# GpSimd's order in the first feed-forward: the next group's statistics ahead of this group's residual sums, with two once-normalised tiles

## The chip, the cores and the metric

The kernel runs on one core of a Trainium2 chip. The metric is the device time of one launch in microseconds (us); less is better. Five engines work side by side, each through its own list of instructions and in order: TensorE (PE in the rows, PEld for its weight loads), VectorE (DVE), ScalarE (ACT), GpSimd (POOL) and SyncE (SP), which starts transfers. They meet only at semaphores. SBUF is the on-chip memory that all of them read, and PSUM is the memory in which TensorE leaves its sums.

## The reference

A tensor x of 64 tiles, each of 128 tokens by 128 features, goes through four blocks of cross-attention and feed-forward. Each of the eight steps is added to x. The change touches the second step only, the first feed-forward (`L0_ffn`). It normalises an input that the caller has already normalised, so the normalisation is done twice:

```python
h0 = _layernorm(x)                       # once-normalised
# _L0_ffn_ref(h0, ...):
residual = h0
h = (h0 - mean(h0)) * rsqrt(var(h0) + EPS) * ln_gamma + ln_beta   # twice-normalised
w1 = dequant(fc1_q, fc1_scales)          # 128 x 512
y = silu(h @ w1 + fc1_bias)
z = y @ dequant(fc2_q, fc2_scales) + fc2_bias
x = x + (residual + 0.5 * z)
```

So three things are added to x in this step: the once-normalised tile h0 (the residual), half of the bias, and half of the product. The halving is folded into the weights and the bias beforehand.

## The kernel before

x stays in SBUF as one tile `x` of 128 partitions (tokens) by 64 by 128. Each step walks over it in 16 groups of 4 tiles (`GROUPS`, `GT`), 512 columns at a time. The first feed-forward is the class `SiluFfn`, whose walk is in its parent `Hidden`. For one group g the work is this, in the order of the data:

- VectorE takes the means and variances of the four tiles (`vector_stats`, L186 and L191) into `ln_mean_var`. There is only one such buffer.
- GpSimd turns them into the factors of both normalisations (`pool`, six small instructions of 128x4, L204 to L210). L205 and L210 are powers of -1/2. Each of the six waits for the one before. The results are in `ln_rstd` and `ln_rstd2` (the rows call both ln_rstd).
- VectorE writes the once-normalised tile `f_once` (L239, four instructions of 128x128) and from it the twice-normalised tile `z` (L244, four more). This is `vector_z`.
- TensorE transposes z (`turn_z`, L985), ScalarE copies it out with gamma and beta (`f_zt`, L1051), and VectorE splits it into a high part (L1086, a cast) and a low part (L1088, a difference of two SBUF tiles).
- TensorE makes the hidden layer from high and low parts (`hidden`, L86 to L88, twelve products for a group), ScalarE applies silu (L1062), and TensorE makes the output (`output`, L1013).
- GpSimd adds `f_once` to x (L221) and then the bias (L224). This is `pool_bias`. VectorE adds the output to x (`add_output`, L1099), which reads one operand from PSUM.

The groups are staggered. In one turn of the loop TensorE takes hidden(g+1), the transposes of z(g+2) and output(g). VectorE takes z(g+2), the statistics of g+3, the split of g+2 and the sum of output(g), in this order. The order is written out by hand in `tensor_walk`, `vector_walk`, `scalar_walk` and `gpsimd`, and nothing else sets it. GpSimd takes one group after the other, first `pool(g)` and then `pool_bias(g)`, so its factors for the next group wait behind the two sums of this one. VectorE may not write `f_once` again before L221 has read it (the semaphore `once_added`).

`for_groups` is the helper that unrolls a loop by two so that buffers in pairs have a constant index `par`. The loop over GpSimd's groups used a plain loop before.

Of the kernel before, what the change touches and what calls it, by code (L numbers as in the profile page):

```python
# [25 lines left out]
F32 = mybir.dt.float32  # L26
F32R = mybir.dt.float32r
BF16 = mybir.dt.bfloat16
ALU = mybir.AluOpType
# [4 lines left out]
P = 128  # L34
# [4 lines left out]
GT = 4  # L39
GROUPS = BATCH // GT  # L40
# [6 lines left out]
class Counter:  # L47


    def __init__(self, sem, credit=0):  # L50
        self.sem, self.credit, self.base = sem, credit, credit
# [21 lines left out]
def for_groups(eng, body, peel=1):  # L73


    with eng.Fori(0, GROUPS // 2 - peel) as i:
        body(2 * i, 0, 2 * peel)
        body(2 * i + 1, 1, 2 * peel)
    for left in range(2 * peel - 1, -1, -1):
        body(GROUPS - 1 - left, 1 - left % 2, left)  # L80
# [15 lines left out]
class Core:  # L96
# [24 lines left out]
    def sb(self, ctx, name, shape, dt):  # L121
        return ctx.enter_context(self.nc.sbuf_tensor(name, shape, dt))
# [24 lines left out]
class Chain:  # L147
# [5 lines left out]
    def step(self, eng, ins):  # L153
        ins.then_inc(self.claim.sem, 1)
        self.n += 1
        eng.wait_ge(self.claim.sem, self.claim.at(self.n))


class LayerNorm:
# [51 lines left out]
            if self.once is None:  # L211
                step(eng.tensor_tensor(c.rstd[:, :], c.rstd[:, :], c.rstd2[:, :], ALU.mult))

    def pool_bias(self, eng, g):
        if self.bias is None:
            return
        c = self.core
        eng.wait_ge(self.z_ready.sem, self.z_ready.at(GT * g + GT))
        xg = c.x[:, ds(GT * g, GT), :]
        if self.once is not None:  # L220
            eng.tensor_tensor(xg, xg, self.once[:, :, :], ALU.add).then_inc(self.once_added.sem, 1)  # L221
            eng.wait_ge(self.once_added.sem, self.once_added.at(g + 1))
            eng.sem_inc(self.pool_seen.sem, 1)
        eng.tensor_tensor(xg, xg, self.bias[:, :].unsqueeze(1).broadcast_to([P, GT, P]), ALU.add)\  # L224
           .then_inc(self.bias_added.sem, 1)

    def vector_z(self, eng, g):

        c = self.core
        eng.wait_ge(self.rstd_step.sem, self.rstd_step.at(self.pool_steps * g + self.pool_steps))  # L230
        for k in range(GT):
            xk = c.x[:, ds(GT * g + k, 1), :].rearrange("p a d -> p (a d)")
            if self.once is None:
                eng.tensor_scalar(self.dest(g, k), xk, c.mean_var[:, k, 0:1], c.rstd[:, k:k + 1],
                                  ALU.subtract, ALU.mult).then_inc(self.z_ready.sem, 1)
                continue
            if k == 0 and not (isinstance(g, int) and g == 0):
                eng.wait_ge(self.once_added.sem, self.once_added.at(g))
            eng.tensor_scalar(self.once[:, k, :], xk, c.mean_var[:, k, 0:1], c.rstd[:, k:k + 1],  # L239
                              ALU.subtract, ALU.mult).then_inc(self.once_ready.sem, 1)  # L240
        if self.once is not None:
            for k in range(GT):
                eng.wait_ge(self.once_ready.sem, self.once_ready.at(GT * g + k + 1))
                eng.tensor_scalar(self.dest(g, k), self.once[:, k, :], c.rstd2[:, k:k + 1], None, ALU.mult)\  # L244
                   .then_inc(self.z_ready.sem, 1)


# [56 lines left out]
class SavedLayerNorm(LayerNorm):  # L304
# [11 lines left out]
    def pool(self, eng, g):  # L316
        pass

    def vector_z(self, eng, g):
        for k in range(GT):  # L320
            b = GT * g + k
            eng.tensor_scalar(self.dest(g, k), self.core.x[:, ds(b, 1), :].rearrange("p a d -> p (a d)"),
                              self.batch.mean_of(b), self.batch.rstd_of(b), ALU.subtract, ALU.mult)\
               .then_inc(self.z_ready.sem, 1)


class Phase:
# [5 lines left out]
    def gpsimd(self, eng):  # L333
        pass
# [605 lines left out]
class Hidden(Phase):  # L940
# [161 lines left out]
    def vector_walk(self, eng):  # L1102
        self.ln.vector_z(eng, 0)
        self.split_zt(eng, 0, 0)
        self.ln.vector_stats(eng, 1)
        self.ln.vector_z(eng, 1)
        self.apply_gates(eng, 0, 0)
        self.split_zt(eng, 1, 1)
        self.ln.vector_stats(eng, 2)

        def step(g, par, left):
            if left > 1:
                self.ln.vector_z(eng, g + 2)
            if left > 2:
                self.ln.vector_stats(eng, g + 3)
            if left > 0:
                self.apply_gates(eng, g + 1, 1 - par, (0, 1))
            if left > 1:
                self.split_zt(eng, g + 2, par)
            if left > 0:  # L1120
                self.apply_gates(eng, g + 1, 1 - par, (2, 3, 4))
            self.add_output(eng, g, par)

        for_groups(eng, step, 2)
        eng.wait_ge(self.added.sem, self.added.at(GROUPS))
        eng.sem_inc(self.done.sem, 1)

    def gpsimd(self, eng):
        eng.wait_ge(self.before.sem, self.before.at(1))
        self.ln.pool(eng, 0)  # L1130
        self.wait_bias(eng)
        self.ln.pool_bias(eng, 0)
        with eng.Fori(1, GROUPS) as g:
            self.ln.pool(eng, g)
            self.ln.pool_bias(eng, g)


class SiluFfn(Hidden):
# [5 lines left out]
    def __init__(self, core, before):  # L1144
        self.core = core
        self.i = {k[len("L0_ffn_"):]: v for k, v in core.ins.items() if k.startswith("L0_ffn_")}
        C = self.F // P
        sb, ctx = core.sb, ExitStack()
        self.affine = sb(ctx, "f0_gb", [P, 2], F32)
        self.b1 = sb(ctx, "f0_b1", [P, C], F32)  # L1150
        self.bias = sb(ctx, "f0_b2", [P, P], F32)
        self.q1 = sb(ctx, "f0_q1", [P, self.F], mybir.dt.int32)
        self.q2 = sb(ctx, "f0_q2", [P, C, P], mybir.dt.int32)
        self.s1 = sb(ctx, "f0_s1", [P, self.F], F32)
        self.w2 = self.s2 = sb(ctx, "f0_w2", [P, C, P], F32)
        self.w1 = [sb(ctx, f"f0_w1{h}", [P, self.F], F32R) for h in ("hi", "lo")]
        self.once = sb(ctx, "f0_once", [P, GT, P], F32)
        self.setup(before, [P] * C, ACT.Silu, LayerNorm(core, True, self.bias, once=self.once))
        self.buffers(ctx, "f0_")
        ctx.close()  # L1160
        self.loaded = core.claim("w_loaded", 16 * 8)
        self.prep = core.claim("prep_step", 6)
# [1385 lines left out]
```

## Time and profile before

| | us |
|---|---|
| median of 3 runs | 3059.89 |
| lowest and highest of them | 3056.15 and 3061.35 |
| span of the profiled execution, first to last instruction | 3055.5 |
| TensorE's mean granted clock in it, share of full speed | 0.917 |

A run's time is that of the launch. The span leaves out what lies before the first and behind the last instruction. The profiled execution's own launch time is not listed apart; its span is 0.65 us under the fastest of the three runs and 4.4 us under their median. A time worked out from the trace is therefore a difference of two spans, and it is added to the median.

Of this span the first feed-forward takes some 160 us: its first statistics start at 729.86 and its last sum into x ends at 891.87. A row of the timeline gives the start, the length, the engine, the line, the operation, output and inputs, the number of instructions that are merged into the row, and in brackets how long the engine was idle before it and whom it waited for. A merged row names the start of its first instruction, and its length runs to the end of its last.

### The profile page before, as it was taken

What the parts mean: (1) busy time and instruction counts of PE and PEld (TensorE: products, weight loads), DVE (VectorE), ACT (ScalarE), POOL (GpSimd) and SP (SyncE); (2) the same over time, 40 slices, a digit from 0 to 9 for tenths busy, and PEclk for the clock granted to TensorE, in tenths of its full rate; (3) what the DMA queues carried; (4) which work ended last, traced back from release to release, by engine and by line L of the source; (5) the groups of instructions that cost most, each with busy time, mean ns of one, the idle gap of its engine ahead of it and who ended that gap; (6) DMA issues with size and microseconds to landing.
All of it is one profiled execution on the core that took longest, in us unless ns stands there. A gap on an engine that the chain in (4) does not pass through costs nothing.

```text
span 3055.5 us, 58066 instructions
## 1 busy us (share of the span) xinstructions
PE 2622.0 (86%) x17377; PEld 2252.0 (74%) x17378; DVE 2034.5 (67%) x4748; ACT 1653.6 (54%) x3673; POOL 426.9 (14%) x572
## 2 busy tenths in 40 slices
PE   6999999996879999413589999999966997869998
PEld 5888888884768988301378888888865786668887
DVE  4888888886647777679846666666665444655554
ACT  4666666663336666225566666666623433425554
POOL 1011100111630111230000000000000102302223
PEclk9999999998999999755779999999968998969999
DMA  4000000000000000000000000000000000020000
GB/s 105 1 0 0 0 0 0 0 1 15 0 13 1 0 0 0 8 0 0 21 5 1 0 0 0 0 0 0 1 9 0 0 0 4 0 85 8 14 14 22
DMA packets 36054, 25.06 MB, mean 8 GB/s; under 512 B 10300, under 2 KB 32332, under 8 KB 35852
## 3 DMA queue, kind: packets, MB, share of 16 engines
q1 hardware_dynamic: 35980, 24.12, 2.9%
q8 instruction: 41, 0.67, 0.1%
q14 instruction: 33, 0.27, 0.0%
HBM read 19.92 MB, written 4.19 MB: 8 GB/s over the span
## 4 chain that ended last, share of the span: by engine, by line
PE 75%; DVE 9%; issue 6%; ACT 4%; POOL 3%; DMA 1%; DVEq 1%; POOLq 0%; SPq 0%; ACTq 0%
PE ps_o L637 11%; PE ps_t L614 11%; PE ps_s L626 11%; PE ps_p L86 6%; PE ps_p L88 6%; PE ps_p L87 6%; PE ps_t L2214 2%; PE ps_o L2214 2%; PE ps_o L1013 2%; PE ps_s L86 2%; PE ps_t L1013 2%; ACT a_vals_t L734 1%; PE ps_s L88 1%; PE ps_s L87 1%; DVE f_rng L1414 1%
## 5 line engine op out<-in xcount | busy, mean ns | idle before, releaser
L854 DVE TENSOR_REDUCE a_sm<-a_e 128x16 f32<-128x1232 f32 (+1 forms) x192 | 234.6, 1222 | 401.7 <-ACT a_e L762 400.8
L754 ACT ACTIVATE a_val<-ps_t 128x512 f32<-128x512 f32 (+1 forms) x448 | 223.2, 507 | 400.5 <-PE ps_t L614 399.0
L637 PE MATMUL ps_o<-a_val,a_pt 128*128 128x128 f32 (+2 forms) x3200 | 390.6, 276 | 4.0 <-DVE x L868 2.6
L637 PEld LDWEIGHTS ps_o<-a_val,a_pt 128*128 128x128 f32 (+2 forms) x3200 | 382.5, 192 | 12.3 <-DVE x L868 3.1
L626 PE MATMUL ps_s<-a_keys,a_zt 128*128 128x308 f32 (+1 forms) x1024 | 365.0, 488 | 4.6 <-DVE a_e L846 2.4
L734 ACT ACTIVATE a_vals_t<-ps_p 128x308 f32<-128x308 f32 x616 | 264.4, 430 | 84.2 <-PE ps_p L88 84.0
L734 ACT ACTIVATE a_keys<-ps_p 128x308 f32<-128x308 f32 x614 | 263.2, 429 | 58.5 <-PE ps_p L88 58.4
L614 PE MATMUL ps_t<-ident,a_e 128*128 128x128 f32 (+1 forms) x1600 | 265.2, 278 | 32.6 <-DVE a_e L862 16.0
L626 PEld LDWEIGHTS ps_s<-a_keys,a_zt 128*128 128x128 f32 x1024 | 185.0, 190 | 117.5 <-issue 101.3
L614 PE MATMUL ps_t<-ident,a_vals_t 128*128 128x128 f32 (+1 forms) x1600 | 251.8, 273 | 9.5 <-ACT a_val L754 9.5
L86 PE MATMUL ps_p<-ct_hi,a_vo_hi 96*128 (+1 forms) x616 | 241.5, 392 | 5.6
L86 PE MATMUL ps_p<-ct_hi,a_mt_hi 96*128 (+1 forms) x614 | 243.3, 396 | 0.0
L754 ACT ACTIVATE a_pt<-ps_t 128x512 f32<-128x512 f32 (+1 forms) x448 | 226.1, 507 | 29.9 <-PE ps_t L614 29.5
L862 DVE TENSOR_TENSOR a_e<-a_e,a_rs 128x1232 f32<-128x1232 f32 (+1 forms) x192 | 235.7, 1228 | 6.6
L614 PEld LDWEIGHTS ps_t<-ident,a_e 128*128 128x128 f32 (+1 forms) x1600 | 190.8, 139 | 56.8 <-issue 24.7
L762 ACT ACTIVATE a_e<-a_e 128x1232 f32<-128x1232 f32 (+1 forms) x192 | 204.7, 1066 | 5.0 <-DVE a_e L846 4.8
L204 POOL TENSOR_TENSOR ln_var<-ln_mean_var,eps 128x4 f32<-128x4 f32 x96 | 24.9, 260 | 1302.6 <-DVE ln_mean_var L191 1255.6
L614 PEld LDWEIGHTS ps_t<-ident,a_vals_t 128*128 128x128 f32 (+1 forms) x1600 | 190.0, 138 | 19.5 <-ACT a_val L754 18.5
L88 PE MATMUL ps_p<-ct_hi,a_mt_lo 96*128 (+1 forms) x614 | 188.9, 308 | 0.0
L87 PE MATMUL ps_p<-ct_lo,a_mt_hi 96*128 (+1 forms) x614 | 188.6, 307 | 0.0
L88 PE MATMUL ps_p<-ct_hi,a_vo_lo 96*128 (+1 forms) x616 | 187.2, 304 | 0.0
L87 PE MATMUL ps_p<-ct_lo,a_vo_hi 96*128 (+1 forms) x616 | 187.2, 304 | 0.0
(358 smaller groups left out, 5651.9 us busy)
## 6 DMA issues: line engine op xcount, KB each, us to landing
x<-in_x_dram SPq DMA_DIRECT2D x8, 512.0 KB, 7.5
out_dram<-x SPq DMA_DIRECT2D x8, 512.0 KB, 3.2
f_wf<-in_L_ffn_W_dram SPq DMA_DIRECT2D x1, 2048.0 KB
f_b<-in_L_ffn_b_dram SPq DMA_DIRECT2D x1, 2048.0 KB, 13.4
ctx_rows<-in_ctx_dram SPq DMA_DIRECT2D x4, 462.0 KB
a_wq<-in_L_xattn_Wq_dram SPq DMA_DIRECT2D x2, 512.0 KB
a_wo<-in_L_xattn_Wo_dram SPq DMA_DIRECT2D x2, 512.0 KB
f_w<-in_L_ffn_W_dram SPq DMA_DIRECT2D x3, 256.0 KB
```

The costliest lines, as they stand in the source:

```text
L86: eng.matmul(out, lhs[0], rhs[0], start=start, stop=False)
L87: eng.matmul(out, lhs[0], rhs[1], start=False, stop=False)
L88: return eng.matmul(out, lhs[1], rhs[0], start=False, stop=stop)
L614: mm = eng.transpose(c.ps_t[0:w, slot, (i % GT) * P:(i % GT + 1) * P], src[:, P * i:P * i + w], c.ident[:, :])
L626: eng.matmul(o, zt, keys[:, h0:h0 + nh, :], start=True, stop=True)\
L637: mm = eng.matmul(c.ps_o[:, (k % 2) * P:(k % 2 + 1) * P], self.pt[0:w, i, :], self.val[0:w, i, :], start=(i == 0), stop=(i == self.chunks ...
L734: eng.activation(dst[:, par, :, h, :], src.rearrange("p (b k) -> p b k", b=GT), ACT.Copy)\
L754: mm = eng.activation(dst[:, i0:full, :], src[:, 0:full - i0, :], ACT.Copy)
L762: eng.activation(self.e[:, par, :], self.e[:, par, :], ACT.Exp).then_inc(self.exp_ready.sem, 1)
L854: eng.tensor_reduce(self.sm[:, :], e, AX.X, ALU.add).then_inc(st.sem, 1)
L862: eng.tensor_tensor(e, e, bc(self.rs[:, :], KEYS), ALU.mult).then_inc(self.probs_ready.sem, 1)
L1013: mm = eng.matmul(o, self.hid[0:w, par, c, k * P:(k + 1) * P], self.w2[0:w, c, :], start=c == 0, stop=c == self.C - 1 and not self.gated)
```

## The change

Three edits go together. The first moves instructions on GpSimd: `pool(g+1)` now stands ahead of `pool_bias(g)`. The second gives `f_once` two halves, one for even and one for odd groups, since L221 now reads a group's tile while VectorE may already write the next group's. The third moves VectorE's wait for `once_added` one group back, to match. In all other feed-forwards and attentions the code does what it did.

```diff
-    def pool_bias(self, eng, g):
+    def pool_bias(self, eng, g, par=0):
...
-            eng.tensor_tensor(xg, xg, self.once[:, :, :], ALU.add).then_inc(self.once_added.sem, 1)
+            eng.tensor_tensor(xg, xg, self.once[:, par], ALU.add).then_inc(self.once_added.sem, 1)
...
-            if k == 0 and not (isinstance(g, int) and g == 0):
-                eng.wait_ge(self.once_added.sem, self.once_added.at(g))
-            eng.tensor_scalar(self.once[:, k, :], xk, c.mean_var[:, k, 0:1], c.rstd[:, k:k + 1],
+            if k == 0 and not (isinstance(g, int) and g < 2):
+                eng.wait_ge(self.once_added.sem, self.once_added.at(g - 1))
+            eng.tensor_scalar(self.once[:, par, k, :], xk, c.mean_var[:, k, 0:1], c.rstd[:, k:k + 1],
...
-        self.ln.vector_z(eng, 1)
+        self.ln.vector_z(eng, 1, 1)
...
-                self.ln.vector_z(eng, g + 2)
+                self.ln.vector_z(eng, g + 2, par)
...
         self.ln.pool(eng, 0)
         self.wait_bias(eng)
-        self.ln.pool_bias(eng, 0)
-        with eng.Fori(1, GROUPS) as g:
-            self.ln.pool(eng, g)
-            self.ln.pool_bias(eng, g)
+
+        def step(g, par, left):
+            if left > 0:
+                self.ln.pool(eng, g + 1)
+            self.ln.pool_bias(eng, g, par)
+
+        for_groups(eng, step)
...
-        self.once = sb(ctx, "f0_once", [P, GT, P], F32)
+        self.once = sb(ctx, "f0_once", [P, 2, GT, P], F32)
```

How GpSimd's list reads at the head of this step, from the last of group 0's six instructions on, before:

```order
L210 TENSOR_TENSOR ln_rstd<-ln_var,neg_half 128x4 [waits rstd_step]
L221 TENSOR_TENSOR x<-x,f_once 128x512 [waits z_ready,prep_step,rstd_step]
L224 TENSOR_TENSOR x<-x,f_b 128x512 [waits once_added]
L1133 UNCONDITIONAL_BRANCH
L1133 ISA
L204 TENSOR_TENSOR ln_var<-ln_mean_var,eps 128x4 [waits aggr_ready]
```

and in the changed kernel:

```order
L210 TENSOR_TENSOR ln_rstd<-ln_var,neg_half 128x4 [waits rstd_step]
L76 UNCONDITIONAL_BRANCH [waits prep_step,rstd_step]
L76 ISA
L204 TENSOR_TENSOR ln_var<-ln_mean_var,eps 128x4 [waits aggr_ready]
L201 ISA
L205 TENSOR_TENSOR ln_rstd<-ln_var,neg_half 128x4 [waits rstd_step]
```

The two sums of group 0 (L221, L224) stood ahead of the loop, whose body begins with L204. Now the loop begins at once with the factors of group 1, and the sums of group 0 come behind them.

At the end of the loop over the groups GpSimd's list read before as follows (the address register is set by the ISA row):

```order
L201 REGISTER_ALU
L221 ISA [waits z_ready,rstd_step]
L221 TENSOR_TENSOR x<-x,f_once 128x512
L222 REGISTER_ALU
L224 TENSOR_TENSOR x<-x,f_b 128x512 [waits once_added]
L1133 REGISTER_ALU
L1133 COMPARE_AND_BRANCH
```

and in the changed kernel the list ends, behind the loop, with the last group's factors and then two pairs of sums, those of groups 14 and 15:

```order
L210 TENSOR_TENSOR ln_rstd<-ln_var,neg_half 128x4 [waits rstd_step]
L221 TENSOR_TENSOR x<-x,f_once 128x512 [waits z_ready,rstd_step]
L224 TENSOR_TENSOR x<-x,f_b 128x512 [waits once_added]
L221 TENSOR_TENSOR x<-x,f_once 128x512 [waits z_ready]
L224 TENSOR_TENSOR x<-x,f_b 128x512 [waits once_added]
```

On VectorE no arithmetic instruction moves. At group 1 the wait of the first once-normalisation changes, as this piece of the difference shows:

```order
 L191 BN_AGGR ln_mean_var<-ln_stats 128x2 [waits stats_ready]
 L191 BN_AGGR ln_mean_var<-ln_stats 128x2 x3
-L239 TENSOR_SCALAR f_once<-x,ln_mean_var,ln_rstd 128x128 [waits once_added,rstd_step]
+L239 TENSOR_SCALAR f_once<-x,ln_mean_var,ln_rstd 128x128 [waits rstd_step]
 L239 TENSOR_SCALAR f_once<-x,ln_mean_var,ln_rstd 128x128 x3
 L244 TENSOR_SCALAR z<-f_once,ln_rstd 128x128 [waits once_ready] x4
```

Only the wait for `once_added` is gone there. In the loop it stays and asks for one group less.

## Rows read from the trace of the kernel before

**Rows 1.** The page, its first line.

```profile
span 3055.5 us, 58066 instructions
```

**Rows 2.** The stage table, 781.1 to 868.3, ten groups: busy us of PE, PEld, DVE, ACT, POOL.

```profile
781.10:868.30 87.20, 69.82 (x480) 61.40 (x480) 58.15 (x191) 32.03 (x50) 59.01 (x80) 1.00 0.00 0
```

**Rows 3.** The timeline of one group, 781 to 790 (start, length, last: idle before, releaser).

```profile
781.10 0.66 PE L985 MATMUL ps_t<-ident,z 128*128 128x128 f32 x4 [1.80 <-DVE z L244]
781.30 1.27 POOL L221 TENSOR_TENSOR x<-x,f_once 128x512 f32 x1 [2.31 <-DVE z L244]
...
781.98 0.38 DVE L191 BATCH_NORM_AGGREGATE ln_mean_var<-ln_stats 128x2 f32<-128x6 f32 x4 [0.15 <-DVE ln_stats L186]
782.61 0.43 DVE L1086 CAST f_zthi<-f_zt 128x512 fp32r<-128x512 f32 x1 [0.25 <-ACT f_zt L1051]
782.76 1.40 POOL L224 TENSOR_TENSOR x<-x,f_b 128x512 f32 x1 [0.19 <-POOL x L221]
783.07 1.64 DVE L1088 TENSOR_TENSOR f_ztlo<-f_zt,f_zthi 128x512 fp32r<-128x512 f32 x1
784.12 0.65 POOL L204 TENSOR_TENSOR ln_var<-ln_mean_var,eps 128x4 f32<-128x4 f32 x1
...
785.58 0.69 DVE L1099 TENSOR_TENSOR x<-ps_t,x 128x512 f32 x1 [0.86 <-PE ps_t L1013]
...
786.78 1.01 POOL L210 TENSOR_TENSOR ln_rstd<-ln_var,neg_half 128x4 f32<-128x4 f32 x1
...
787.71 0.39 PE L88 MATMUL ps_p<-f_zthi,f_w1lo 128*128 128x512 f32 x1
787.82 1.12 DVE L239 TENSOR_SCALAR f_once<-x,ln_mean_var,ln_rstd 128x128 f32 x4 [1.56 <-POOL ln_rstd L210]
...
788.86 0.87 DVE L244 TENSOR_SCALAR z<-f_once,ln_rstd 128x128 f32<-128x128 f32 x4
...
789.78 0.44 PE L985 MATMUL ps_t<-ident,z 128*128 128x128 f32 x2 [1.68 <-DVE z L244]
```

**Rows 4.** The timeline, groups 2 and 3, stretch 762 to 774.

```profile
763.58 0.92 PE L985 MATMUL ps_t<-ident,z 128*128 128x128 f32 x4 [2.17 <-DVE z L244]
...
769.68 0.69 DVE L1099 TENSOR_TENSOR x<-ps_t,x 128x512 f32 x1 [2.16 <-PE ps_t L1013]
...
770.35 1.12 DVE L239 TENSOR_SCALAR f_once<-x,ln_mean_var,ln_rstd 128x128 f32 x4
...
772.31 0.66 PE L985 MATMUL ps_t<-ident,z 128*128 128x128 f32 x4
```

**Rows 5.** The timeline, the last group's turn of z.

```profile
877.00 0.66 PE L985 MATMUL ps_t<-ident,z 128*128 128x128 f32 x4 [1.69 <-DVE z L244]
```

**Rows 6.** The timeline, group 0's statistics with VectorE idle.

```profile
730.88 0.38 DVE L191 BATCH_NORM_AGGREGATE ln_mean_var<-ln_stats 128x2 f32<-128x6 f32 x4
...
731.40 0.20 POOL L204 TENSOR_TENSOR ln_var<-ln_mean_var,eps 128x4 f32<-128x4 f32 x1 [59.36 <-DVE ln_mean_var L191]
...
733.61 1.01 POOL L210 TENSOR_TENSOR ln_rstd<-ln_var,neg_half 128x4 f32<-128x4 f32 x1
```

**Rows 7.** The view of the tile f_once (lengths in ns: least, median, most).

```profile
L239 DVE TENSOR_SCALAR f_once<-x,ln_mean_var,ln_rstd x64: 336/341/347, 740.5 to 875.8; 128x128 f32 x48, 128x128 f32<-128x128 f32 x16
L244 DVE TENSOR_SCALAR z<-f_once,ln_rstd x64: 277/279/283, 741.5 to 876.7; 128x128 f32<-128x128 f32 x64
```

**Rows 8.** The timeline, last feed-forward: VectorE and GpSimd meet.

```profile
2834.41 1.71 DVE L2306 TENSOR_SCALAR f_z<-x,f_x_mean_var,f_x_rstd 128x128 f32 x2
...
2834.75 1.30 POOL L2147 TENSOR_TENSOR x<-x,f_y 128x512 f32 x1 [0.28 <-POOL f_y L2143]
```

**Rows 9.** The timeline, group 0's cast and group 1's turn.

```profile
744.55 0.99 DVE L1086 CAST f_zthi<-f_zt 128x512 fp32r<-128x512 f32 x1 [2.16 <-ACT f_zt L1051]
...
750.92 1.12 DVE L239 TENSOR_SCALAR f_once<-x,ln_mean_var,ln_rstd 128x128 f32<-128x128 f32 x4 [3.33 <-POOL ln_rstd L210]
```

**Rows 10.** The timeline, last attention: GpSimd's power beside VectorE.

```profile
2552.26 1.02 POOL L205 TENSOR_TENSOR ln_rstd<-ln_var,neg_half 128x4 f32<-128x4 f32 x1
2552.41 0.29 DVE L1976 TENSOR_TENSOR a_wvlo<-a_wv,a_wvhi 96x128 fp32r<-96x128 f32 x1
```

More of the change, by code:

```diff
@@ L225, in pool_bias, with vector_z @@
            .then_inc(self.bias_added.sem, 1)
-    def vector_z(self, eng, g):
+    def vector_z(self, eng, g, par=0):
         c = self.core
@@ L243, in vector_z @@
                 eng.wait_ge(self.once_ready.sem, self.once_ready.at(GT * g + k + 1))
-                eng.tensor_scalar(self.dest(g, k), self.once[:, k, :], c.rstd2[:, k:k + 1], None, ALU.mult)\
+                eng.tensor_scalar(self.dest(g, k), self.once[:, par, k, :], c.rstd2[:, k:k + 1], None, ALU.mult)\
                    .then_inc(self.z_ready.sem, 1)
@@ L317, in pool, with vector_z @@
         pass
-    def vector_z(self, eng, g):
+    def vector_z(self, eng, g, par=0):
         for k in range(GT):
```

## The prediction

> **What bounds the kernel now.** The page gives the whole span [rows 1]. The change touches only the first feed-forward, so I read that stage. The stage table of ten groups of its loop shows TensorE busy for 69.8 us of 87.2 (80%, at the full granted clock), GpSimd for 59.0 (68%) and VectorE for 58.2 (67%) [rows 2]. No engine is full, so something goes round in a ring. The timeline of one group shows the ring [rows 3]. Times below count from the first transpose of a group, T, at 781.10.
>
> - GpSimd starts L221 at T+0.20 and L224 at T+1.66. Only then, at T+3.02, does it start the six small instructions of the next group, though VectorE's last statistic was ready at T+1.26 (781.98 plus 0.38).
> - These six end at T+6.69 (786.78 plus 1.01). VectorE starts L239 at T+6.72, 0.03 later, and the next transpose follows 1.96 after that (787.82 to 789.78), at T+8.68.
> - TensorE had its last hidden product at 787.71 for 0.39, so it was idle for 1.68 of 8.68 and needs 7.0 for a group. The row says that it waited for z.
>
> The ring is thus sums (2.9 us), factors (3.7), burst on VectorE (2.0). From the transpose at 772.31 to the last at 877.00 there are twelve such periods [rows 3, 4, 5]: (877.00 - 772.31) / 12 = 8.72 each.
>
> A second thing in these rows decides this case. L1088, a difference of 512 columns, takes 1.64. It starts at 783.07 while GpSimd's L224 runs, and it ends at 784.71, 0.55 after L224's end at 784.16. GpSimd's L204, which takes 0.20 when VectorE is idle [rows 6], starts at 784.12, takes 0.65, and ends just after L1088. So these instructions take turns and don't overlap. L239 and L244 never meet GpSimd in this stage: their lengths are 336 to 347 ns and 277 to 283 ns, without one outlier [rows 7]. GpSimd stands idle while they run, because it waits for them. The new order changes that.
>
> Do L239 and L244 also take turns with GpSimd? L2306 in the last feed-forward is the same form as L239 (128x128, two scalar columns). There a pair takes 1.71 and ends at 2836.12, 0.07 after the end of GpSimd's L2147 at 2836.05 [rows 8]. GpSimd started 0.34 after the pair did, so it got in between the two, and the second of the pair waited until L2147 had ended. I take it that a burst of eight short instructions can't keep GpSimd out.
>
> **The change, part by part.** Nothing is added or removed in arithmetic. L221 and L224 move behind the next group's six small instructions.
>
> *What the order would free.* The factors of the next group no longer wait for the sums. With last statistic at T+1.26, 0.14 from there to L204 and 3.22 for the six without VectorE beside them [rows 6], they end at T+4.62. The cast L1086 (T+1.51 to T+1.94) falls on the second of the six and may hold it for some 0.13, so T+4.75. VectorE is busy with the sum of the output then: L1099 starts at T+4.48, and L239 follows 0.67 after such a start (769.68 to 770.35, where the factors were ready) [rows 4]. So L239 could start at T+5.15, and the next transpose at 5.15 + 1.96 = T+7.11. That is 0.1 above what TensorE needs. The gain would be 1.61 a group.
>
> *What it collides with.* GpSimd's two sums now start right behind the factors, when VectorE starts its burst. From L210 to L221 I take 0.2: the gap from L221 to L224, which also waits for itself, is 0.19 [rows 3]; the largest of that kind is 0.26 from z to L221. L221 runs from T+4.95 to T+6.22. The first L239 starts at T+5.15 and is held until 6.22, ending 0.08 later. GpSimd starts L224 at 6.41, so the second L239 (0.26 after the first) still gets through, and the third is held until L224 ends at 6.41 + 1.27 = 7.68. It ends at 7.76. Of the burst's 1.96, 0.85 is then done (0.34 for the first and two steps of 0.26), and 1.11 is left. The next transpose is at T+8.87. Against 8.72 that is +0.15 a group, +1.8 for twelve. The stage's gain is lost in the meeting, to within a tenth of a microsecond. Bounds: a gap of 0.1 to 0.26 and a hold of 0 to 0.2 by the cast make the period 8.64 to 9.00, hence -1.0 to +3.4 for twelve.
>
> *The first groups.* They run as a chain without overlap, so the meeting costs more there than the order frees. Where the factors release the burst directly, it takes 0.1 + 1.96 behind L210 now, and 0.2 + 1.27 + 2.65 then (2.65 is the way from L221's end to the transpose, from the last paragraph), 2.06 more; if the first L239 slips in ahead of L221 it is 1.88 more. I take 1.95. Group 1: the cast of group 0, held for 0.99 by L224 where it takes 0.43 otherwise, is free (-0.56), and the burst at 750.92 meets the sums of group 0 (+1.95) [rows 3, 9]: +1.4. Group 2: the difference L1088 of group 1 is free (-0.95: 1.64 against 0.69, the length of L1099 with as many columns) and the burst is held again (+1.95): another +1.0. Group 3: the period before was 772.31 - 763.58 = 8.73, with the sum of the output as late as T+6.10 [rows 4]. The first L239 is then ready at T+6.77 and held by L224 until 7.68, so the transpose is at 7.76 + 1.62 = T+9.38, +0.65; if TensorE's clock is up by then, the sum of the output comes earlier and it is nearer +0.15. I take +0.4. Together +2.8, with 2.2 to 3.3 as bounds.
>
> *The end.* The sums of group 14 now lie on the burst of group 15, which is the twelfth period above. Those of group 15 come behind its z as before, with the split of group 15 beside them. Nothing is late behind that: the last two outputs on TensorE are the cover, longer than 7 us.
>
> *At nothing.* The wait for `once_added` asks for a sum that ended a whole group earlier; without the second half of `f_once` the burst would wait for L221's end and not gain. VectorE's one register instruction more at L238 and one less at L1095 are hidden behind L1099 (0.69); in the open they would cost under 0.1 each. The sum of group g's bias is needed by L1099 of group g only two groups later, and it moves later by 4.8 us, so it never holds it.
>
> The sum: +1.8 + 2.8 = +4.6 us on the span, 3060.1. The profiled execution's span stands 4.4 under the median, so I add the difference to the median: 3064.5.
>
> **The rivals.**
>
> *The port is kept through the powers.* If GpSimd's L205 kept VectorE's L1088 out for its whole 1.02, the difference would end at T+3.37 and not at 2.66, L207 would be held until then, and the factors would end at T+5.08. All behind moves by 0.33: period 9.20, +5.7 for twelve with the same +2.8, 3068.4. Against it: L1976, a difference of two SBUF tiles, starts 0.15 after such a power and takes 0.29, ending 0.58 before the power does [rows 10]. That speaks for a short hold by an instruction of four columns. The Trainium skill, "SBUF — State Buffer", section Who interferes with whom, says that whichever of such a pair issues first gets the shared port pair for the whole instruction and the other fully blocks. By that rule this rival is the forecast and the time 3068.4; the trace agrees for the long sums and, in the one case shown, not for the power. I give it 0.22. Together with what else may be late (the clock of TensorE rising later, as it idles longer in the first groups), slower cases have 0.27.
>
> *The burst gets through.* If eight instructions behind each other keep GpSimd out, or this form takes no turns when GpSimd came first, the period is 7.11: 12 x (7.11 - 8.72) = -19.3, and -1.5 from the cast and the difference in the first groups, 3039. This ends on the other side. It decides if L221 starts after T+7.0 or if L239 keeps its 0.34 beside it. Against it stand the pair of L2306 and the times above. I give it 0.10.
>
> *Only one meeting.* If L221 holds the burst but L224 comes behind it, the transpose is at 6.22 + 0.08 + 1.62 = T+7.92: 12 x -0.80 = -9.6, +0.7 in the first groups, 3051. The gap from L221 to L224 would have to be over 1.6, and it is 0.19. I give it 0.08.
>
> **How the numbers follow.** The forecast has 0.55, with its own range of 3061 to 3067 (from -1.0 + 2.2 to +3.4 + 3.3 on the median). Beside it 0.27 slower and 0.18 faster, as above. Within 0.2% is 6.1 us either way, about what a measurement of this kernel can tell from no change; nearly all of the forecast lies inside, and a little of it beyond (0.04). That makes faster 0.18, same 0.52, slower 0.30. The range leaves out the two faster rivals and the far end of the slower one: 3056 to 3070.
>
> **What would show it.** In the changed kernel's stage the six small instructions of a group should start right behind the last L191 (now 1.8 later), and L221 right behind L210. L239 and L244 should no longer be uniform: in each group two of the eight should be 0.5 to 1.3 long. L1088 should fall from 1.64 to 0.69 and L224 from 1.39 to 1.27. The transposes should be 8.6 to 9.0 apart in the loop, with TensorE's wait for z still 1.6 or more. The forecast is wrong if the period is under 8.5 (the burst gets through, or half of it), or if L1088 stays over 1.2 with L210 later than T+5 (the port kept through the powers).

## The result, and the profile after

Over 20 runs of each, the changed kernel takes 3064.15 us (3059.77 to 3068.49) and the kernel before 3057.45. The ratio is 1.0023, with a 95% interval of 1.0016 to 1.0030: slower by 5 to 9 us, a little more than 0.2%. (Of the runs of before, one, at 5571 us, is left out of the comparison as disturbed.) The prediction was +4.6 us on the kernel before, that is 3064.5, with a range of 3056 to 3070. It gave 0.52 to a change within 0.2% (6.1 us) and 0.30 to slower; the medians are 6.7 us apart, just outside of that band, and the interval of 5 to 9 us lies on both sides of its edge. That 3064.5 stands so close to the measured 3064.15 is partly luck: the forecast was added to a median of 3059.89 from three runs, and over 20 runs the kernel before takes 3057.45, 2.4 less. From there the same +4.6 gives 3062.1. The difference was forecast 2.1 too small, and the two errors cancel.

The first line of the page of the changed kernel, to be read beside [rows 1]:

```profile
span 3062.1 us, 58012 instructions
```

One group of the loop in the timeline of the changed kernel, from one transpose of z to the next, answers to [rows 3]:

```profile
804.80 0.65 PE L985 MATMUL ps_t<-ident,z 128*128 128x128 f32 x4 [1.88 <-DVE z L244]
...
805.29 3.74 PE L1013 MATMUL ps_t<-f_w,f_hid 128*128 128x128 f32 x32
...
805.68 0.38 DVE L191 BATCH_NORM_AGGREGATE ln_mean_var<-ln_stats 128x2 f32<-128x6 f32 x4 [0.15 <-DVE ln_stats L186]
806.14 0.20 POOL L204 TENSOR_TENSOR ln_var<-ln_mean_var,eps 128x4 f32<-128x4 f32 x1 [2.52 <-DVE ln_mean_var L191]
806.30 0.43 DVE L1086 CAST f_zthi<-f_zt 128x512 fp32r<-128x512 f32 x1 [0.24 <-ACT f_zt L1051]
806.42 1.18 POOL L205 TENSOR_TENSOR ln_rstd<-ln_var,neg_half 128x4 f32<-128x4 f32 x1
806.76 0.69 DVE L1088 TENSOR_TENSOR f_ztlo<-f_zt,f_zthi 128x512 fp32r<-128x512 f32 x1
...
808.52 1.01 POOL L210 TENSOR_TENSOR ln_rstd<-ln_var,neg_half 128x4 f32<-128x4 f32 x1
...
809.27 0.69 DVE L1099 TENSOR_TENSOR x<-ps_t,x 128x512 f32 x1 [1.82 <-PE ps_t L1013]
...
809.81 1.29 POOL L221 TENSOR_TENSOR x<-x,f_once 128x512 f32 x1 [0.28 <-POOL ln_rstd L210]
809.88 3.04 DVE L239 TENSOR_SCALAR f_once<-x,ln_mean_var,ln_rstd 128x128 f32 x4
...
811.29 1.28 POOL L224 TENSOR_TENSOR x<-x,f_b 128x512 f32 x1 [0.19 <-POOL x L221]
...
812.84 0.86 DVE L244 TENSOR_SCALAR z<-f_once,ln_rstd 128x128 f32<-128x128 f32 x4
...
813.75 0.34 PEld L985 LDWEIGHTS ps_t<-ident,z 128*128 128x128 f32 x3 [2.38 <-DVE z L244]
```

Count again from the transpose, T, now 804.80. The six small instructions start at T+1.34, 0.08 after the last statistic (before: 3.02). The last of them, L210, ends at T+4.73. Then L221 starts at T+5.01, and in the same tenth of a microsecond VectorE starts its burst, at T+5.08. Its four L239 take 3.04 where they took 1.12. L224 follows L221 at T+6.49. The next transpose is at T+8.95, behind 1.96 of idle time on TensorE (8.95 less the 6.99 in which it is busy, by the stage table below; the row's 2.38 is that of its weight loads). What was freed behind the statistics has been given back in the burst. L1088 now takes 0.69 and no longer 1.64.

The view of the tile f_once in the changed kernel, least, median and most length in ns, answers to [rows 7]:

```profile
L239 DVE TENSOR_SCALAR f_once<-x,ln_mean_var,ln_rstd x64: 332/336/1330, 742.0 to 885.0; 128x128 f32 x48, 128x128 f32<-128x128 f32 x16
L244 DVE TENSOR_SCALAR z<-f_once,ln_rstd x64: 270/274/279, 743.0 to 885.8; 128x128 f32<-128x128 f32 x64
```

One L239 now takes as long as 1330 ns, and 336 in the median. L244 is as before; the loss sits in the one or two L239 of each burst of eight that GpSimd gets ahead of.

The stage table of four periods of the loop in the changed kernel. The columns after the stretch are its length, then the busy us of TensorE, its weight loads, VectorE, ScalarE and GpSimd, then TensorE's granted clock as a share of full speed:

```profile
795.92:804.80 8.88, 7.00 (x49) 6.15 (x49) 6.63 (x20) 3.20 (x5) 5.59 (x8) 1.00 0.00 0
804.80:813.75 8.95, 6.99 (x48) 6.13 (x48) 6.70 (x20) 3.22 (x5) 5.57 (x8) 1.00 0.00 0
813.75:823.05 9.30, 8.61 (x48) 7.77 (x49) 5.42 (x20) 3.15 (x5) 5.49 (x8) 0.82 0.00 0
823.05:832.02 8.97, 6.99 (x49) 6.14 (x49) 6.72 (x20) 3.25 (x6) 5.58 (x8) 1.00 0.00 0
```

The third of the four runs at 0.82, that is partly at the lower level of 1.2 GHz and not at 2.4 GHz, and it is 9.30 long. In the loop 4 of 12 periods are so (9.30 to 9.44); the other 8 are 8.77 to 8.97 and average 8.89. In the profile of the kernel before, all twelve ran at 1.00. This is what the prediction did not have.

### The profile page after: what moved, and what is told of

It reads as the page before. It is cut to its first block, busy times and chain, and to the rows that moved or that the text cites. A ratio compares the mean times of both kernels' runs of the same rounds, so it can differ in the third digit from the quotient of the medians.

```text
span 3062.1 us, 58012 instructions
## 1 busy us (share of the span) xinstructions
PE 2626.4 (86%) x17369; PEld 2257.2 (74%) x17378; DVE 2040.7 (67%) x4748; ACT 1654.3 (54%) x3673; POOL 422.7 (14%) x572
## 4 chain that ended last, share of the span: by engine, by line
PE 76%; DVE 9%; issue 6%; ACT 4%; POOL 2%; DMA 1%; DVEq 1%; SPq 0%; POOLq 0%; ACTq 0%
PE ps_o L637 11%; PE ps_t L614 11%; PE ps_s L626 11%; PE ps_p L86 6%; PE ps_p L88 6%; PE ps_p L87 6%; PE ps_o L1013 2%; PE ps_t L1013 2%; PE ps_t L2217 2%; PE ps_o L2217 2%; PE ps_s L86 2%; ACT a_vals_t L734 1%; PE ps_s L88 1%; PE ps_s L87 1%; DVE f_rng L1417 1%
## 5 line engine op out<-in xcount | busy, mean ns | idle before, releaser
L86 PE MATMUL ps_p<-ct_hi,a_vo_hi 96*128 (+1 forms) x616 | 241.3, 392 | 5.7
L86 PE MATMUL ps_p<-ct_hi,a_mt_hi 96*128 (+1 forms) x614 | 242.7, 395 | 0.0
L204 POOL TENSOR_TENSOR ln_var<-ln_mean_var,eps 128x4 f32<-128x4 f32 x96 | 19.6, 204 | 1354.5 <-DVE ln_mean_var L191 1307.8
```

Of the source, the lines that this page charges most:

```text
L86: eng.matmul(out, lhs[0], rhs[0], start=start, stop=False)
```

## Experiments

Each is an edit of the changed kernel unless it says otherwise. T and period are as above, and all periods are read from the transposes in the loop. In most of these kernels the last period is 0.1 to 0.2 shorter than the others; the ranges given for a period leave it out, except those of the changed kernel and of the spare product. The work behind this step, which no edit touches, took between 2156.8 and 2164.5 us in the profiles, so a difference of two whole spans carries some 4 us either way, and the stretch of the loop is the better measure.

**Both sums cut to four columns.** The residual and the bias of this step are left out of nearly all of x; the order and all waits stay.

```diff
         if self.once is not None:
-            eng.tensor_tensor(xg, xg, self.once[:, par], ALU.add).then_inc(self.once_added.sem, 1)
+            x4 = c.x[:, ds(GT * g, 1), 0:4].rearrange("p a d -> p (a d)")
+            eng.tensor_tensor(x4, x4, self.once[:, par, 0, 0:4], ALU.add).then_inc(self.once_added.sem, 1)
...
+            eng.tensor_tensor(x4, x4, self.bias[:, 0:4], ALU.add).then_inc(self.bias_added.sem, 1)
```

> The changed kernel, but in the first feed-forward GpSimd's two sums L221 and L224 take 4 columns of one tile each instead of 512 (the residual and the bias of this step are left out of nearly all of x). Theory (the two sums and VectorE's burst take turns at SBUF and that alone eats the gain): the burst L239/L244 keeps its 1.96 us and the transposes come every 7.1 to 7.3 us in the loop, against 8.72 before; twelve periods give -17 to -19, the first groups -1, so 18 to 21 us less than before, ratio 0.993 to 0.994. Rival (another ring at 8.9 us, say TensorE with ScalarE and the sum of the output, holds the period): the same time as the changed kernel, ratio 1.002.

Measured: 3030.40 us, ratio 0.9916 (0.9898 to 0.9934). Two periods in the stage table of this kernel:

```profile
788.53:795.56 7.03, 6.96 (x49) 6.14 (x49) 4.78 (x20) 3.17 (x7) 3.38 (x8) 1.00 0.00 0
795.56:802.62 7.06, 6.99 (x48) 6.13 (x48) 4.81 (x20) 3.22 (x7) 3.40 (x8) 1.00 0.00 0
```

The period is 7.03 to 7.10, and TensorE is busy throughout. No other ring holds the stage at 8.9; the rival falls. This is the time at which the order without a meeting would run, and the prediction had 7.11 for it. The whole is 27 us less than before, where 18 to 21 were expected. In the profile the twelve periods give 20.3 and the first groups 3.0, of which 1 was expected; what is left over lies outside of this stage.

**Only the second sum cut to four columns** (the bias is left out).

> The changed kernel, but only the second sum L224 is cut to 4 columns (the bias is left out). Theory: the burst meets L221 alone. The first L239 waits for its end at T+6.22 and the rest runs through, so the period is 7.9 us; 12 x -0.8 = -9.6 and +0.7 in the first groups, some 9 us less than before, ratio 0.997. If each meeting costs the burst one sum's length less what is in flight, this run lies halfway between both sums small and the changed kernel. Rival (no turns at SBUF): the time of the changed kernel, 1.002.

Measured: 3049.46 us, ratio 0.9968 (0.9955 to 0.9980). Two periods in the stage table of this kernel:

```profile
791.32:799.23 7.91, 6.99 (x48) 6.14 (x49) 5.66 (x20) 3.20 (x5) 4.51 (x8) 1.00 0.00 0
799.23:807.23 8.00, 6.96 (x49) 6.14 (x49) 5.75 (x20) 3.20 (x5) 4.50 (x8) 1.00 0.00 0
```

One meeting makes the period 7.95, as the prediction's third case had it (7.92). So the first sum costs 0.90 and the second another 0.94 (8.89 in the changed kernel at full clock): nearly one sum's length less what is already under way, each.

**Two halves of f_once, old order on GpSimd.**

```diff
+        self.ln.pool_bias(eng, 0, 0)
...
         def step(g, par, left):
-            if left > 0:
-                self.ln.pool(eng, g + 1)
-            self.ln.pool_bias(eng, g, par)
+            if not (isinstance(g, int) and g == 0):
+                self.ln.pool(eng, g)
+                self.ln.pool_bias(eng, g, par)
...
```

> The two halves of f_once and the later wait for once_added, but GpSimd in the old order (factors, then sums, group by group). Theory: the wait was never the last to end, so this is the kernel before, within 1.5 us, period 8.72. Rival (part of the loss comes from the second half or the unrolled loop itself): 1 to 3 us slower.

Measured: 3056.24 us, ratio 0.9994 (0.9985 to 1.0003). The second half and the later wait cost and bring nothing. Three periods in the stage table of this kernel:

```profile
773.60:782.49 8.89, 7.00 (x49) 6.14 (x49) 5.82 (x20) 3.20 (x5) 5.90 (x8) 1.00 0.01 2
782.49:791.16 8.67, 8.62 (x48) 7.76 (x48) 5.75 (x20) 2.54 (x5) 5.90 (x8) 0.80 0.00 0
791.16:800.04 8.88, 7.00 (x48) 6.14 (x48) 5.82 (x20) 3.87 (x7) 5.90 (x8) 1.00 0.00 0
```

This gives more than was asked. The middle one has a granted clock of 0.80, as some periods of the changed kernel have, and it is not longer for it. Over most of the loop the periods alternate between 8.88 and 8.67 here; those of its own kind take 8.67 or 8.68 at 1.00 as well, and the three low ones 8.67, 8.67 and 8.71. In the old order the ring runs over GpSimd, and TensorE only fills its idle time.

**A seventh small instruction in the factors, in the kernel before.** It changes no result.

```diff
             step(eng.tensor_tensor(c.rstd2[:, :], c.ln_var[:, :], c.neg_half[:, :], ALU.pow))
+            if self.once is not None:
+                step(eng.tensor_tensor(c.ln_var[:, :], c.mean_var[:, :, 1], c.rstd[:, :], ALU.mult))
```

> The kernel before with a seventh small instruction of 128x4 in GpSimd's chain of factors in the first feed-forward (it changes no result). Its ring gets 0.28 us longer: period 9.0, 15 times +0.28 = +4.2 us, ratio 1.0014. TensorE then idles 2.0 us a group. Theory on the clock: some periods of the loop are granted less than 1.00, as in the changed kernel. Since the ring of the kernel before doesn't pass through TensorE's output, low periods cost it little more. Rival on the clock (it falls for another reason than the idle time a group): all periods from the fourth group on at 1.00, as before.

Measured: 3063.64 us, ratio 1.0016 (1.0007 to 1.0025). Three periods in the stage table of this kernel:

```profile
783.76:792.72 8.96, 7.00 (x48) 6.14 (x49) 5.82 (x20) 3.22 (x5) 6.11 (x9) 1.00 0.00 0
792.72:801.81 9.09, 8.62 (x48) 7.77 (x49) 5.83 (x20) 2.94 (x5) 6.11 (x9) 0.81 0.00 0
801.81:810.78 8.97, 7.00 (x49) 6.14 (x49) 5.83 (x20) 3.48 (x6) 6.11 (x9) 1.00 0.00 0
```

Each period is longer by the instruction, 8.96 to 9.09, whatever the clock (9.02 on average, where it was 8.72: 0.30 for the expected 0.28). The low periods are there too, 4 of 12 at 0.81 or 0.82, and again they cost next to nothing (0.05 at most beside a period of the same kind).

**A spare product on TensorE ahead of its wait for z.**

```diff
     def turn_z(self, eng, g, par):
         c = self.core
+        if isinstance(self, SiluFfn):
+            for _ in range(1):
+                eng.matmul(c.bank(4), self.w2[:, 0, :], self.w2[:, :, :].rearrange("p c d -> p (c d)"), start=True, stop=True)
         eng.wait_ge(self.ln.z_ready.sem, self.ln.z_ready.at(GT * g + GT))
```

> The changed kernel with one spare product of 128x512 into an unused PSUM bank ahead of TensorE's wait for z, in each group of the first feed-forward. In the changed kernel's trace every third period of the loop has the granted clock at 0.82 and is 9.30 to 9.44 us long, the others at 1.00 are 8.86 to 8.97. Theory (the clock falls because TensorE idles 1.9 us a group instead of 1.7): with the gap nearly filled the clock stays at 1.00, all periods are 8.9, 2 to 3 us less than the changed kernel, ratio to before 1.0013 to 1.0016. Rival (the clock falls for another reason): the low periods stay and the time is that of the changed kernel or a little more, 1.0023 or above.

Measured: 3060.48 us, ratio 1.0009 (1.0000 to 1.0017). Three periods in the stage table of this kernel:

```profile
804.78:813.73 8.95, 7.85 (x50) 6.51 (x50) 6.70 (x20) 3.21 (x5) 5.57 (x8) 1.00 0.00 0
813.73:822.60 8.87, 7.86 (x51) 6.52 (x51) 6.62 (x20) 3.20 (x5) 5.58 (x8) 1.00 0.00 0
822.60:831.55 8.95, 7.86 (x51) 6.52 (x51) 6.70 (x20) 3.21 (x5) 5.56 (x8) 1.00 0.00 0
```

All twelve periods are at 1.00 and 8.77 to 8.95 long. From the first transpose to the last it is 139.7 us against 142.1 in the changed kernel, though TensorE does more. That leaves the meeting alone, and the two intervals (1.0000 to 1.0017, 1.0016 to 1.0030) barely touch. So the lower clock takes 2.4 us of the changed kernel's loss by the profiles, as expected (2 to 3); by the ratios it is some 4, which the two intervals leave open between 1 and 8 (an estimate). Why it falls is less sure: TensorE's idle time drops from 1.9 to 1.1 us a period here and the clock stays up, but the kernel with the two halves had low periods at 1.7 to 1.9 us of idle time and the profile of before, at 1.7 to 1.8, had none.

**Each sum in four instructions of 128 columns.**

```diff
-            eng.tensor_tensor(xg, xg, self.once[:, par], ALU.add).then_inc(self.once_added.sem, 1)
+            for k in range(GT):
+                xk = c.x[:, ds(GT * g + k, 1), :].rearrange("p a d -> p (a d)")
+                ins = eng.tensor_tensor(xk, xk, self.once[:, par, k, :], ALU.add)
+            ins.then_inc(self.once_added.sem, 1)
...
+                ins = eng.tensor_tensor(xk, xk, self.bias[:, :], ALU.add)
```

> The changed kernel, with each of GpSimd's two sums cut into four instructions of 128 columns. Same work, same place. Theory (turns are taken instruction by instruction): an instruction of the burst now waits for at most some 0.3 us, a quarter of a sum, and the eight short ones go in between the eight quarters. If GpSimd's quarters follow each other every 0.35 us, the burst ends at about T+8.0 and the period is 8.1 (8.0 to 8.5): 12 x -0.6 = -7, first groups about +1, so 2 to 7 us less than before, ratio 0.998 to 0.9995. Rival (GpSimd keeps its turn over its whole queue): period 8.9 or more, ratio 1.002 or more.

Measured: 3054.00 us, ratio 0.9986 (0.9977 to 0.9995). The meeting in the timeline of this kernel (L223 and L230 are the two sums, L248 and L253 the burst):

```profile
805.29 1.71 POOL L223 TENSOR_TENSOR x<-x,f_once 128x128 f32 x4 [0.29 <-POOL ln_rstd L210]
805.36 1.72 DVE L248 TENSOR_SCALAR f_once<-x,ln_mean_var,ln_rstd 128x128 f32 x4
...
807.00 1.54 DVE L253 TENSOR_SCALAR z<-f_once,ln_rstd 128x128 f32<-128x128 f32 x4
807.18 1.70 POOL L230 TENSOR_TENSOR x<-x,f_b 128x128 f32 x4 [0.18 <-POOL x L223]
```

The period is 8.23 to 8.33. Four quarters and four instructions of the burst take 1.71 and 1.72 side by side: one of each in turn, some 0.4 us a pair, and neither waits for a whole sum. Turns are taken by the instruction, not by the queue. The work and its place are those of the changed kernel, and by the two ratios it is some 11 us faster.

**The two sums apart.** The bias sum stays behind the factors, and the sum of f_once waits until the next group's z is written; the sum of the output now waits for it.

```diff
             if left > 0:
                 self.ln.pool(eng, g + 1)
-            self.ln.pool_bias(eng, g, par)
+            self.ln.pool_bias_first(eng, g)
+            if left > 0:
+                eng.wait_ge(self.ln.z_ready.sem, self.ln.z_ready.at(GT * g + 2 * GT))
+            self.ln.pool_once_last(eng, g, par)
```

> The order of the changed kernel, but the two sums are taken apart: the bias sum stands right behind the factors, as now, and the sum of f_once waits for the next group's z, so that it runs beside the statistics. VectorE's sum of the output waits for the f_once sum. With the bias sum cut to 4 columns the period was 7.95 us; here one full sum still meets the burst, so the same 7.9 to 8.1 (the second sum ends just when the statistics are ready). 12 x -0.75 = -9, first groups +0 to +1: 7 to 10 us less than before, ratio 0.997 to 0.998. Rival (GpSimd's total work or a second meeting with the cast and the factors gives it back): period 8.3 or more, ratio above 0.999.

Measured: 3048.83 us, ratio 0.9970 (0.9958 to 0.9983). Two periods in the stage table of this kernel:

```profile
799.43:807.42 7.99, 7.00 (x49) 6.14 (x49) 5.83 (x20) 3.30 (x5) 5.41 (x8) 1.00 0.00 0
807.42:815.32 7.90, 6.97 (x49) 6.14 (x49) 5.74 (x20) 3.26 (x5) 5.41 (x8) 1.00 0.00 0
```

The period is 7.90 to 8.00. All the work is done, and it is as fast as the kernel in which the bias sum was nearly left out. Where a sum stands decides, not that it is there.

**The same, with the bias sum in four instructions.**

> As the kernel with the sums apart, and the bias sum, the one that still meets the burst, is cut into four instructions of 128 columns. Eight quarters stretched the burst by 8.28 - 7.11 = 1.2 us a period; four should stretch it by 0.6 and give 7.7. 12 x -1.0 = -12, first groups about 0: 11 to 13 us less than before, ratio 0.996. Rival (the stretch is not in proportion, since the second sum now runs into the factors): 8.0, no better than the uncut one.

Measured: 3044.35 us, ratio 0.9957 (0.9943 to 0.9971), 13 us less than before. Two periods in the stage table of this kernel:

```profile
803.95:811.53 7.58, 6.99 (x49) 6.14 (x49) 5.42 (x20) 3.22 (x6) 5.87 (x11) 1.00 0.00 0
811.53:819.19 7.66, 6.99 (x48) 6.13 (x48) 5.50 (x20) 3.38 (x6) 5.86 (x11) 1.00 0.00 0
```

The period is 7.56 to 7.67. This is the shortest period of all versions that compute everything.

**The bias on TensorE.** The sum of f_once stands as in the last two kernels, so no sum meets the burst; four products per group of a row of ones by the bias open the output sums.

```diff
         for k in tiles:
             o = self.obank(par)[:, k * P:(k + 1) * P]
+            if isinstance(self, SiluFfn):
+                eng.matmul(o, self.ones[0:1, :], self.bias[0:1, :], start=True, stop=False)
```

> The bias sum leaves GpSimd: TensorE adds it in PSUM with one product per tile of a row of ones by the bias (four more per group, 0.12 us each by the output products' pace, 0.5 a group). GpSimd's only sum left, that of f_once, waits for the next group's z and meets no burst. TensorE then needs 7.0 + 0.5, and the sum of the output comes 0.5 later, so the period is 7.5 to 7.6. 12 x -1.15 = -14, first groups -1.5: 14 to 16 us less than before, ratio 0.995. This is the best of the versions if the meeting is the whole cause. Rival (a ring not seen yet at 7.9, e.g. L1088 beside the f_once sum): -9.

Measured: 3075.53 us, ratio 1.0060 (1.0046 to 1.0074). A miss. From the timeline of this kernel:

```profile
799.19 0.48 PE L1025 MATMUL ps_t<-f_b,f_ones 1*128 1x128 f32 x2
...
803.69 0.48 PE L1025 MATMUL ps_t<-f_b,f_ones 1*128 1x128 f32 x2
...
805.02 0.47 PE L86 MATMUL ps_s<-f_zthi,f_w1hi 128*128 128x512 f32 x1
...
806.03 1.11 DVE L252 TENSOR_SCALAR f_once<-x,ln_mean_var,ln_rstd 128x128 f32 x4
```

L252, the first half of the burst, is back at 1.11, so the meeting is gone as expected. But from a group's first bias product to its first hidden product behind the outputs it is 5.83 (799.19 to 805.02). The outputs alone take 3.49 there, as in the group of the changed kernel above, from 805.29 to its next L86 at 808.78. Four bias products thus cost 2.34, about 0.6 each and not 0.12. Part of that was a misreading: the kernel issues 16 output products for a group and the rows count 32, two records for each product, so the pace of the output products is 3.49 / 16 = 0.22, and 0.12 is that of a record. TensorE becomes the bound, and the period is 9.37 to 9.44. The profiled execution took 3063.79 and the four others 3074.11 to 3078.26; where those 11 us lie, no profile shows.

**The same over all 128 rows.** The row of ones becomes a tile of 1/128, and the bias tile has the bias in each row.

```diff
-                eng.matmul(o, self.ones[0:1, :], self.bias[0:1, :], start=True, stop=False)
+                eng.matmul(o, self.ones[:, :], self.bias[:, :], start=True, stop=False)
```

> As the kernel with the bias on TensorE, but the product is over all 128 rows: a tile of 1/128 in place of the row of ones, by the bias tile, which holds the bias in each of its 128 rows. With one row each such product cost 0.6 us and not 0.12 (a period of 9.38 to 9.44 with TensorE busy throughout). Theory (the products of one row among those of 128 rows cost the change of rows, not their columns): now 0.12 each, period 7.5 to 7.6, no meeting with the burst; 12 x -1.15 = -14 and -1.5 in the first groups, 14 to 16 us less than before, ratio 0.995. Rival (any product that opens a PSUM sum ahead of the others costs 0.6): period 9.4, ratio 1.003 to 1.006.

Measured: 3045.75 us, ratio 0.9961 (0.9947 to 0.9974). From the timeline of this kernel:

```profile
800.16 0.39 PE L1025 MATMUL ps_o<-f_b,f_ones 128*128 128x128 f32 x2
...
804.55 0.48 PE L86 MATMUL ps_s<-f_zthi,f_w1hi 128*128 128x512 f32 x1
...
805.58 1.11 DVE L252 TENSOR_SCALAR f_once<-x,ln_mean_var,ln_rstd 128x128 f32 x4
```

From the first bias product to the first hidden product it is 4.39, so a bias product over 128 rows costs (4.39 - 3.49) / 4 = 0.22, as much as an output product. The rival falls. The period is 7.83 to 7.90 with TensorE busy throughout, its 7.0 and four times 0.22. That is faster than before by 13 us, short of the 14 to 16 expected, since 0.12 stood for 0.22. TensorE is now the bound. The period is longer than with the bias sum in four instructions, but the times of the two kernels can't be told apart.

## Why the prediction was right, and where its size was off

**The ring and what the order frees: right.** L210 ends at T+4.73 (predicted 4.75), and L239 could start at T+5.08 (5.15). Without the sums the period is 7.05 (7.11); there the ring and TensorE's own 7.0 fall together.

**The meeting: right, by place and size.** L221 starts at T+5.01 (4.95), L224 at 6.49 (6.41). At full clock the next transpose is 8.89 away on average (8.87). Both sums meet the burst, 0.90 and 0.94 each by the two kernels with sums cut.

**The clock: the term that was missing.** Twelve periods took 886.15 - 777.61 = 108.5 us against 104.7, +3.9 where +1.8 stood. Eight of them, at full clock, give +1.3 and fit. The other four give +2.5, of which 1.9 is the step from 8.89 to 9.35. The sum treated TensorE's clock as 1.00 throughout the loop, since all its rows showed that. It did have L1099 ahead of the burst, at T+4.48, but at that clock only. Here is what a low period looks like in the timeline of the changed kernel:

```profile
814.50 5.12 PE L1013 MATMUL ps_o<-f_w,f_hid 128*128 128x128 f32 x32
...
818.60 1.28 POOL L221 TENSOR_TENSOR x<-x,f_once 128x512 f32 x1 [0.19 <-POOL ln_rstd L210]
...
819.86 0.69 DVE L1099 TENSOR_TENSOR x<-ps_o,x 128x512 f32 x1 [3.15 <-PE ps_o L1013]
...
820.07 1.29 POOL L224 TENSOR_TENSOR x<-x,f_b 128x512 f32 x1 [0.19 <-POOL x L221]
...
820.49 1.72 DVE L239 TENSOR_SCALAR f_once<-x,ln_mean_var,ln_rstd 128x128 f32 x4
```

The output's 32 records take 5.12 and not 3.74 as in the group shown above, so the sum of the output L1099 is at 819.86, T+6.11 and not T+4.47. The burst waits behind it on VectorE. L221 is over by then, and L224 alone meets the burst (L239 at 1.72 for four). The new order thus has two ways to lose, and a period pays one or the other: early output and two meetings, 8.9, or late output and part of one, 9.35. The old order paid for neither. The kernels with the two halves and with a seventh small instruction show it: at 0.80 to 0.82 their periods are 8.67 and 9.09, as long as those of the same kind at 1.00. What the change did besides moving instructions is to put TensorE's output into the ring. A low period pays for only part of its clock: TensorE is busy for 1.6 us longer in it (8.6 for 7.0), and it is 0.46 longer, since one meeting falls away.

**The first groups: right in kind, too small by 1.0.** From the first transpose to the fourth it is 33.6 us against 29.8, +3.8 with +2.8 predicted. Group 1 gave +1.5 (1.4), group 2 +1.4 (1.0), group 3 +0.8 (0.4). In the timeline of the changed kernel:

```profile
755.89 1.10 PE L985 MATMUL ps_t<-ident,z 128*128 128x128 f32 x4 [3.19 <-DVE z L244]
...
757.91 0.43 DVE L1086 CAST f_zthi<-f_zt 128x512 fp32r<-128x512 f32 x1 [2.07 <-ACT f_zt L1051]
...
774.87 0.69 DVE L1099 TENSOR_TENSOR x<-ps_t,x 128x512 f32 x1 [3.71 <-PE ps_t L1013]
775.48 1.28 DVE L239 TENSOR_SCALAR f_once<-x,ln_mean_var,ln_rstd 128x128 f32 x4
```

The transposes at 755.89 take 1.10 and not 0.66, at the lower clock, and the cast behind them is at T+2.02 and not at T+1.57 (754.44 in the kernel before): 0.45 of group 2. In group 3 the sum of the output is at T+6.83 and not at T+6.10, so L239 starts at T+7.44 and not at T+6.77, and L224, which ends at 775.92, holds it for 0.17 only. Of that +0.8, 0.67 is the clock and 0.17 the meeting. The prediction named the clock as the open end of this term and took the middle.

**At nothing: right.** The two halves and the moved wait give 0.9994. From the last transpose to the last sum into x it is 14.87 in both kernels.

**The rivals.** The port kept through the powers (0.22) would have ended near the measured time, but by another mechanism, and it is wrong: L1088 starts at 806.76, while L205 runs from 806.42 to 807.60, and takes its plain 0.69; L210 ends at T+4.73 and not 5.08. The rule of the Trainium skill, "SBUF — State Buffer", section Who interferes with whom, says that the first of such a pair holds the port for the whole instruction and the other fully blocks (the page says it of VectorE's two-port forms, and that an instruction with two SBUF inputs contends with GpSimd's reads). It fits the sums of 512 columns in every period here. It does not fit the power of 4 columns. The burst that gets through and the single meeting don't happen in the changed kernel; each exists as an experiment, near the period that the prediction gave for it (7.05 for 7.11, and 7.95 for 7.92).

The sum with the clock put in is +2.0 for the periods at full clock, 1.9 for the low ones and 3.8 for the first groups, +7.7 from the first transpose to the last, as the trace has it (142.1 against 134.5). The median moved by 6.7 and the span by 6.6. The two don't check each other more closely than this: ahead of the loop the profile of the changed kernel is 1.5 us later (its first transpose at 744.03, before 742.53), and what comes behind this step took 2.6 less in it, by the scatter told above.

## What to carry to other kernels

When GpSimd waits for VectorE and VectorE for GpSimd, their SBUF instructions can't meet; an order that removes the wait lets them meet, and a burst of short instructions is held once by each long one. Put the long one beside work that does not take turns (here the statistics, whose rows are 0.86 and 0.38 with a sum beside them and without), or cut it into pieces of the burst's size: apart and cut, the same work gives 0.9957 where the plain reordering gave 1.0023.

Before trusting a ring's period, ask which engines the new ring passes through. A lower clock on TensorE cost at most 0.05 us a period as long as TensorE was beside the ring, and 0.46 once its output was in it. Here that was the part of the loss which no row of the kernel before shows.

## What the runs showed of the hardware

A product of one row among products of 128 rows cost 0.6 us, the same product over 128 rows 0.22 us, as much as an output product, at full clock and with the same 128 columns.

A GpSimd power on 128x4 takes 1.02 us, but a difference of two SBUF tiles on VectorE that starts 0.34 into it is not held (0.69), nor is the cast L1086 where it starts behind the power (0.43 at 788.32, 0.22 into it). The other way round the power is held. In the nine periods of the changed kernel in which the cast was 0.11 under way, the power took 1.18 to 1.20, and in the three in which the cast came behind it, 1.02. Where the power started 0.10 or 0.11 behind the difference, it took 1.47 (766.93 in the kernel before, 801.74 in the last experiment).

TensorE's granted clock differed between profiles with the same work and nearly the same idle time (all twelve periods at 1.00 in the profile of before, 3 of 12 at 0.80 with the two halves), so one profile does not tell whether a stage keeps its clock.
